# GpSimd instead of SyncE counts the landed row blocks of a graph layer

## The chip, the core and the metric

The kernel runs on one core of a Trainium2 chip. The metric is the device time of one execution in microseconds. A core has five engines with a queue of instructions each: TensorE (matrix products; its weight loads are shown as a unit of their own, PEld), VectorE (DVE), ScalarE (ACT), GpSimd (POOL) and SyncE (SP). They meet only through semaphores: an instruction adds to one, and another engine's queue waits until it holds a value. Transfers (DMA) add 16 to a semaphore when they have landed.

## What is computed

A relational graph layer over 6250 nodes, 200,000 edges and 16 edge types, followed by a layer of 16 experts of which each node takes two:

```python
w_full = jnp.einsum('rb,bdo->rdo', w_comp, weight)
x_rel = jnp.einsum('nd,rdo->rno', feat, w_full)
msg = x_rel[etypes, src] * norm
agg = jax.ops.segment_sum(msg, dst, num_segments=N)
out = agg + h_bias + feat @ loop_weight
return jax.nn.relu(out)
```

Here `feat` is the layer-normed `x` (6250 x 256), `src` and `dst` are the edge's ends, and the edges come sorted by `dst`. The result is added to `x`; the expert layer (gate, top 2 of 16, two products, sum, layer norm) is computed behind it and added in the same way. The change lies in the graph layer.

## The kernel before

The edges are cut into 1568 blocks of 128, the nodes into windows of 16. A step is one block and one window: a matrix `S` with, for each edge and each of the 8 bases, the coefficient of the edge in the column of its node, times the 128 gathered feature rows of the block, added up in a bank of PSUM for the window. There are 1960 steps, seven of which make a turn, so 280 turns.

Each engine has its part of the function `graph_layer`, and they run beside one another:

GpSimd gathers. One indirect DMA (L1069) fetches the 128 feature rows of one block into one of 56 places of a ring in SBUF, `rows`. The first 28 gathers are issued by the stage before the layer, 1540 by the layer itself, in groups of 14 with a list of indices each (L1045), eight groups to a pass of the loop. Ahead of each gather, `landed` (L1047 to L1050) waits until the gather three before it has landed, so no more than three are in flight. The landing semaphores are `s_row`, eight of them in rotation. Then `landed` adds 1 to `s_paced`, which nothing reads. Ahead of each group, L1058 waits until TensorE has done the turns (`s_P`) that read the places to be overwritten.

SyncE first sends for the layer's weights (L1017 to L1022). Then it waits for the row blocks one after the other on the same `s_row` and adds 1 to `s_in` for each (L1025, L1026). Between blocks 392, 616, 896 and 1120 (the third number in `CHUNK`, times 56) it leaves that loop, waits until VectorE has made the `S` of turn 36, 72, 108 or 140 (`s_S`, L1031), and sends for a piece of the late coefficients, 128 rows of 7 or 8 KB (L1033), into the part of `coefS` that those turns have used up. VectorE needs the first of these pieces at turn 141.

VectorE makes four `S` in rotation (L1150), up to three turns ahead of TensorE, and does the layer norm of each tile of 256 nodes that is complete.

TensorE waits per turn for the cleared bank, for `s_in` to reach the last block of the turn (L1275) and for `S` (L1276, L1277), and multiplies (L1278). Where a tile of nodes is complete, it does the tile's product with the basis weights in between (`tile_product`, L1231 to L1244).

ScalarE copies the banks out and clears them, and moves the tiles' rows from and to HBM.

At the end of the layer all engines meet at a barrier (L974), where the slowest is VectorE with the last tile.

Of the kernel before, what the change touches and what calls it, by code (L numbers as in the profile page):

```python
# [38 lines left out]
NBLK = 1568  # L39
# [9 lines left out]
TURNS = STEPS // U  # L49
NS = 4  # L50
# [5 lines left out]
FIRST = TURNS // 2  # L56
LATE = FIRST * U
NEAR = -(-LATE // CS)
CHUNK = [(0, 36, 7), (36, 36, 11), (72, 36, 16), (108, 32, 20)]
assert sum(n for _, n, _ in CHUNK) == TURNS - FIRST and all(n % NS == 0 for _, n, _ in CHUNK) and FIRST % NS == 0  # L60
ZC = B * WIN
BANK = 512
NB = 4
# [15 lines left out]
RB = 56  # L79
GB = 14  # L80
ROWS = 8
AHEAD = 3
IB = 2 * (RB // GB)
EG = 2
CTL_PART = (84, 72, 64, 60)
assert NBLK % RB == 0 and RB % GB == 0 and RB % ROWS == 0 and AHEAD < ROWS and sum(CTL_PART) == TURNS and all(n % NS == 0 for n in CTL_PART)
assert all(t + n <= 8 * i <= TURNS for t, n, i in CHUNK)


SLOTS = (N * K + X * (P - 1)) // P  # L90
# [9 lines left out]
def at_least_one(e, loaded, held):  # L100

    for to, of in zip(held, loaded):
        e.reg_alu(to, of, 1, ALU.max)
    return held
# [74 lines left out]
def later(i):  # L179

    return not isinstance(i, int) or i > 0
# [786 lines left out]
def graph_layer(nc, d, a, ctl, pairs, room, wend, srcT, dstS, wgtS, coefS, ident, wb, lw, hb, gw, s_w, logit, choice, mean, rstd, idx, rows, s_row):  # L968
# [5 lines left out]
    with ctx:  # L974
        def sb(name, shape, dt=F32):
            return ctx.enter_context(nc.sbuf_tensor(name, shape, dt))

        def sem(name):
            return ctx.enter_context(nc.semaphore(name))

        zero = sb("zero", [P, H])
        S = [sb(f"S{h}", [P, U * ZC]) for h in range(NS)]
        z = sb("z", [P, TW * H])
        node = z[:, 0:WIN]
# [15 lines left out]
        node_h = psH[:, 2 * U * WIN:(2 * U + 1) * WIN]  # L1000

        s_in = sem("rows_in")
        s_pool, s_turn, s_paced, s_zr, s_node = sem("pool"), sem("pool_turn"), sem("pool_paced"), sem("zero"), sem("node")
        s_late = [sem(f"late{k}") for k in range(len(CHUNK))]
        s_hot, s_S, s_P, s_clear = sem("hot"), sem("steps_ready"), sem("turn_done"), sem("cleared")
        s_z, s_tp, s_ev = sem("z_done"), sem("tp_done"), sem("tp_out")
# [6 lines left out]
        @blk.sync  # L1013
        def _(e):


            for c in range(HC):  # L1017
                e.dma_start(wb[:, c, :, :], a["L0_gnn_weight"].rearrange("b (c p) o -> c p b o", p=P)[c, :, :, :]).then_inc(s_w, 16)
            e.dma_start(lw[:, :, :], a["L0_gnn_loop_weight"].rearrange("(c p) o -> p c o", p=P)).then_inc(s_w, 16)
            e.dma_start(hb[:, :], a["L0_gnn_h_bias"].partition_broadcast(P)).then_inc(s_w, 16)  # L1020
            e.dma_start(choice[0][:, :], a["L0_ffn_gate_b"].partition_broadcast(P)).then_inc(s_gb, 16)
            e.dma_start(gw[:, :, :], a["L0_ffn_gate_w"].rearrange("(c p) e -> p c e", p=P)).then_inc(s_w, 16)  # L1022
            def rows_in(i):
                for j in range(RB):
                    e.wait_ge(s_row[j % ROWS], i * (RB // ROWS * 16) + (j // ROWS + 1) * 16)  # L1025
                    e.sem_inc(s_in, 1)  # L1026
            i0 = 0
            for k, (t, n, i1) in enumerate(CHUNK):
                with e.Fori(i0, i1) as i:
                    rows_in(i)  # L1030
                e.wait_ge(s_S, t + n)  # L1031
                c = slice(t * U * B, (t + n) * U * B)
                e.dma_start(coefS[:, c], d.coef[:, c]).then_inc(s_late[k], 16)  # L1033
                i0 = i1
            with e.Fori(i0, NBLK // RB) as i:
                rows_in(i)

        @blk.gpsimd
        def _(e):
            ch = Chain(e, s_pool)  # L1040
            regs, room_held = ([e.alloc_register(f"{n}{q}") for q in range(IB)] for n in ("room", "room_held"))
            last = NBLK // (IB * GB) - 1

            def list_in(group, q):
                ch.add(e.tensor_copy(idx[:, q * GB:(q + 1) * GB], srcT[:, bass.ds(group * GB, GB)]))  # L1045

            def landed(i, n):  # L1047

                e.wait_ge(s_row[n % ROWS], i * (IB * GB // ROWS * 16) + (n // ROWS + 1) * 16)
                e.sem_inc(s_paced, 1)  # L1050

            def blocks(i):
                e.load(regs, room[0:1, bass.ds(i * IB, IB)])
                free = at_least_one(e, regs, room_held)
                for q in range(0 if later(i) else EG, IB):
                    if later(i) or q >= RB // GB:

                        e.wait_ge(s_P, free[q])  # L1058
                        e.sem_inc(s_turn, 1)
                    if later(i) or q > EG:  # L1060
                        ch.wait()
                    if q < IB - 1 or not isinstance(i, int) or i < last:
                        list_in(i * IB + q + 1, (q + 1) % IB)
                    else:
                        e.sem_inc(s_turn, 1)
                    for u in range(GB):
                        at = (q * GB + u) % RB
                        landed(i, q * GB + u - AHEAD)
                        e.indirect_dma_start(rows[:, at * H:(at + 1) * H], None, d.feat, bass.IndirectOffsetOnAxis(ap=idx[:, q * GB + u:q * GB + u + 1], axis=0)).then_inc(s_row[at % ROWS], 16)  # L1069
            e.iota(choice[1][:, :], [[1, X]], base=-X, channel_multiplier=0, allow_small_or_imprecise_dtypes=True).then_inc(s_xno, 1)  # L1070
            e.iota(node.rearrange("p (m n) -> p m n", m=2), [[1, 2], [2, WIN // 2]], base=0, channel_multiplier=0, allow_small_or_imprecise_dtypes=True).then_inc(s_node, 1)
            blocks(0)
            with e.Fori(1, last) as i:
                ch.base, ch.n = IB * i - EG, 0
                blocks(i)
            ch.base, ch.n = IB * last - EG, 0
            blocks(last)

        @blk.vector
        def _(e):  # L1080
# [73 lines left out]
            def four(i, t0, c0):  # L1154

                for h0 in range(0, NS, 2):
                    pair(i, t0, c0, h0)
                    if t0:
                        look(i * (NS // 2) + (t0 + h0) // 2)
            four(0, 0, 0)  # L1160
            with e.Fori(0, FIRST // NS - 1) as i:
                four(i, NS, NS)
            for k, (c0, n, _) in enumerate(CHUNK):
                e.wait_ge(s_late[k], 16)
                with e.Fori(0, n // NS) as i:
                    four(i, FIRST + c0, c0)
# [811 lines left out]
def gnn(nc, d, a, ident, sent, got, s_row, logit, choice, mean, rstd):  # L1978
# [3 lines left out]
    with ctx:  # L1982
# [21 lines left out]
        with pre:  # L2004
# [9 lines left out]
            expand(nc, d, wcd, halfs, win_n, ident, tables, wend, pairs, jcol, wcol, spread, dstS, wgtS, coefS, got, s_feat, srcT, idx, rows, s_row)  # L2014
        wb, lw, hb, gw = sb("wb", [P, HC, B, H]), sb("lw", [P, HC, H]), sb("hb", [P, H]), sb("gw", [P, HC, X])
        graph_layer(nc, d, a, ctl, pairs, room, wend, srcT, dstS, wgtS, coefS, ident, wb, lw, hb, gw, s_w, logit, choice, mean, rstd, idx, rows, s_row)


# [54 lines left out]
```

## Time and profile before

| | |
|---|---|
| Median of 3 runs | 2842.06 us (2833.11 to 2845.28) |
| The profiled execution | 2844.61 us |
| Its span, first to last instruction | 2842.7 us |
| TensorE (PE) busy | 2224.4 us, 78% |
| VectorE (DVE) busy | 967.4 us, 34% |
| ScalarE (ACT) busy | 654.3 us, 23% |
| GpSimd (POOL) busy | 1815.4 us, 64% |
| Graph layer | from about 158 us to 2240 us of the span |

Busy time is time in which the engine itself works; instructions of its queue alone (waits, counts on semaphores, branches, the issue of a DMA by SyncE or ScalarE) are not in it. Such instructions carry a q behind the engine's name (SPq, POOLq) and can be listed by their line, with their count and the start of the first and the last. A wait appears as idle time ahead of the next instruction of that engine, put down to the one that ended it; "issue" is idle time for which the profile shows no such one. Times in the views count from the start of the span.

### The profile page before, as it was taken

Reading aid. Unit: us, or ns where it says so; the run is one execution under the profiler, and the core shown is the slowest. Engines: PE = TensorE matmul, PEld = TensorE weight load, DVE = VectorE, ACT = ScalarE, POOL = GpSimd, SP = SyncE. Lnnn points to the kernel's source line nnn. Section 1 sums busy time; section 2 is a strip of 40 time slices with the busy share of each in tenths; the row PEclk is TensorE's granted clock in tenths of the full one; section 3 lists DMA queues with packets and bytes.
Section 4 is the critical chain, followed back from the end, with each engine's and each line's share of the span. In section 5 each row is a group of like instructions: output and inputs, shape, how many; then the busy total and the mean of one; then the engine's idle time right before and its main releaser. Section 6 shows DMA issues by size and latency. Waiting matters only on the chain. (4 is left out here: it accounts for less than half of the span.)

```text
span 2842.7 us, 43421 instructions
## 1 busy us (share of the span) xinstructions
PE 2224.4 (78%) x11549; PEld 1849.9 (65%) x11550; DVE 967.4 (34%) x2172; ACT 654.3 (23%) x1539; POOL 1815.4 (64%) x2000
## 2 busy tenths in 40 slices
PE   1779999999988888876776768557655579999987
PEld 0567787877776666664664646445444379999975
DVE  6733333342332322222222212112112453333347
ACT  2522323232222211111110101001000233333345
POOL 0557777777777777777777777777777035555544
PEclk9999999999999989998898878789777799999998
DMA  6544444344333434334333333333333552222246
GB/s 210 160 146 119 121 118 123 116 120 134 116 117 111 129 111 116 111 112 122 109 109 109 118 107 108 108 100 114 103 103 94 187 182 70 70 70 70 70 131 220
DMA packets 146270, 338.66 MB, mean 119 GB/s; under 512 B 36674, under 2 KB 56290, under 8 KB 146051
## 3 DMA queue, kind: packets, MB, share of 16 engines
q0 software_dynamic: 89296, 245.33, 29.5%
q1 hardware_dynamic: 39311, 59.54, 6.1%
q10 hardware_dynamic: 17588, 32.88, 3.5%
q8 instruction: 36, 0.59, 0.1%
q14 instruction: 39, 0.32, 0.0%
HBM read 292.84 MB, written 47.97 MB: 120 GB/s over the span
## 5 line engine op out<-in xcount | busy, mean ns | idle before, releaser
L1069 POOL DMA_INDIRECT rows<-feat,idx x1540 | 1468.1, 953 | 548.9 <-issue 462.5
L1278 PE MATMUL psW<-rows,S 128*128 x3920 | 1065.1, 433 | 413.8 <-SPq L1026 380.8
L1278 PEld LDWEIGHTS psW<-rows,S 128*128 128x128 f32 x3920 | 842.1, 219 | 632.7 <-issue 495.0
L1150 DVE TENSOR_TENSOR S<-psHere,coefS 128x896 f32<-128x896 f32 x280 | 301.6, 1090 | 1379.0 <-PE psW L1278 1372.4
L1338 ACT COPY z<-psW 128x512 f32<-128x512 f32 x196 | 114.9, 586 | 1461.3 <-PE psW L1278 1460.6
L1244 PE MATMUL psG<-wb,zT 128*128 128x256 f32 (+1 forms) x1600 | 353.5, 379 | 0.0
L1244 PEld LDWEIGHTS psG<-wb,zT 128*128 128x128 f32 (+1 forms) x1600 | 300.6, 188 | 44.7
L1729 PE MATMUL psH<-xT,w1x 128*128 128x128 f32 x1840 | 226.8, 277 | 0.3
L1680 POOL DMA_INDIRECT expert_rows<-os,at_rows x114 | 114.0, 1000 | 171.3 <-DVE os L1788 171.3
L1729 PEld LDWEIGHTS psH<-xT,w1x 128*128 128x128 f32 x1840 | 216.5, 193 | 2.0 <-issue 1.9
L1738 PE MATMUL psO<-w2s,hT 128*128 x912 | 215.7, 379 | 0.0
L1702 ACT ACTIVATE hT<-psH,b1T 128x128 f32<-128x128 f32 x460 | 131.5, 368 | 315.6 <-PE psH L1729 315.6
L1676 POOL DMA_INDIRECT xs<-y_rows,at_rows x116 | 115.0, 991 | 100.7 <-POOLq L1408 56.6
L1738 PEld LDWEIGHTS psO<-w2s,hT 128*128 128x128 f32 x912 | 164.6, 190 | 17.6
L1788 DVE TENSOR_TENSOR os<-psO,b_b 128x256 f32<-128x256 f32 x114 | 48.4, 425 | 236.9 <-PE psO L1738 236.4
L1231 PE MATMUL psZ<-ident,z 128*128 128x128 f32 x784 | 113.8, 283 | 13.5 <-ACT zT L1352 8.8
L1340 ACT COPY psW<-zero 128x512 f32<-128x512 f32 x196 | 115.6, 590 | 6.2
L1352 ACT COPY zT<-psZ 128x512 f32<-128x512 f32 x196 | 108.1, 589 | 18.4 <-PE psZ L1231 18.4
L1231 PEld LDWEIGHTS psZ<-ident,z 128*128 128x128 f32 x784 | 83.7, 141 | 36.1 <-ACT zT L1352 20.1
L1772 DVE COPY w1x<-w1s 128x1024 f32 x116 | 86.1, 742 | 0.0
L1898 PE MATMUL psSum<-g,dg 128*128 128x256 f32 x200 | 56.0, 405 | 17.3 <-DMA g<-expert_rows 17.1
L1141 DVE TENSOR_TENSOR psHere<-dstS,psHere 128x224 f32<-128x224 f32 (+1 forms) x140 | 55.3, 395 | 31.5 <-DVE S L1150 25.1
(284 smaller groups left out, 1442.1 us busy)
## 6 DMA issues: line engine op xcount, KB each, us to landing
rows<-feat,idx POOLq DMA_INDIRECT x1568
g<-expert_rows SPq DMA_DIRECT2D x24, 512.0 KB, 5.5
w1s<-in_L_ffn_w SPq DMA_DIRECT2D x8, 1024.0 KB, 10.0
w2s<-in_L_ffn_w SPq DMA_DIRECT2D x16, 512.0 KB, 10.1
feat<-rows SPq DMA_DIRECT2D x24, 256.0 KB, 3.0
fts<-feat ACTq DMA_DIRECT2D x24, 256.0 KB, 2.8
h<-in_x ACTq DMA_DIRECT2D x24, 256.0 KB
y_rows<-y ACTq DMA_DIRECT2D x24, 256.0 KB
```

What stands on the lines that cost most here:

```text
L1069: e.indirect_dma_start(rows[:, at * H:(at + 1) * H], None, d.feat, bass.IndirectOffsetOnAxis(ap=idx[:, q * GB + u:q * GB + u + 1], axis=0) ...
L1150: e.tensor_tensor(S[h0 + h][:, :].rearrange("p (s b n) -> p s b n", s=U, b=B), both[:, h * U:(h + 1) * U, :].unsqueeze(2).to_broadcast([P, ...
L1231: last = e.transpose(to[:, k * P:(k + 1) * P], z[:, w * H + c * P:w * H + (c + 1) * P], ident[:, :])
L1244: last = e.matmul(psG[0:Q, m * H:(m + 1) * H], zT[:, at:at + Q], wb[:, c, b, :], start=False, stop=(c == HC - 1 and b == B - 1))
L1278: last = e.matmul(psW[:, bass.ds(bank[u], H)], S[h][:, u * ZC:(u + 1) * ZC], rows[:, bass.ds(slot[u], H)], start=False, stop=True, skip_gr ...
L1338: e.copy(z[:, 2 * k * H:2 * (k + 1) * H], bank).then_inc(s_z, 1)
L1340: e.copy(bank.rearrange("p (w o) -> p w o", w=2), zero[:, :].unsqueeze(1).to_broadcast([P, 2, H])).then_inc(s_clear, 1)
L1676: e.indirect_dma_start(xs[n % XS][:, :], None, d.y, bass.IndirectOffsetOnAxis(ap=at_rows[:, n, 0:1], axis=0)).then_inc(s_in[n % XS], 16)
L1680: e.indirect_dma_start(d.two, bass.IndirectOffsetOnAxis(ap=at_rows[:, n + 4, 1:2], axis=0), os_[n % 2][:, :], None).then_inc(s_out[n % 2], 16)
L1702: last = e.activation(hT[k][:, c * P:(c + 1) * P], psH[k][:, c * P:(c + 1) * P], ACT.Relu, bias=b1T[:, bass.ds(ex * FC + c, 1)])
L1729: last = e.matmul(psH[k][:, f * P:(f + 1) * P], w1x[k][:, c * F + f * P:c * F + (f + 1) * P], xT[k][:, c * P:(c + 1) * P], start=(c == 0), ...
L1738: last = e.matmul(psO[k][:, 0:H], hT[k][:, c * P:(c + 1) * P], w2s[:, bass.ds(ex, 1), c, :].rearrange("p e f -> p (e f)"), start=(c == 0), ...
```

## The change

The order of the counts moves. `landed` on GpSimd adds to `s_in` instead of `s_paced`, which goes. Since `landed` begins with block 25, GpSimd counts the 25 blocks before that ahead of its first list, and the last three behind its last gather. SyncE keeps the weights and the four loads of late coefficients, each of which it issues as soon as VectorE has made the `S` of the turn in question; the third number of `CHUNK` goes with the loops.

```diff
-CHUNK = [(0, 36, 7), (36, 36, 11), (72, 36, 16), (108, 32, 20)]
+CHUNK = [(0, 36), (36, 36), (72, 36), (108, 32)]
...
-            def rows_in(i):
-                for j in range(RB):
-                    e.wait_ge(s_row[j % ROWS], i * (RB // ROWS * 16) + (j // ROWS + 1) * 16)
-                    e.sem_inc(s_in, 1)
-            i0 = 0
-            for k, (t, n, i1) in enumerate(CHUNK):
-                with e.Fori(i0, i1) as i:
-                    rows_in(i)
+            for k, (t, n) in enumerate(CHUNK):
                 e.wait_ge(s_S, t + n)
                 c = slice(t * U * B, (t + n) * U * B)
                 e.dma_start(coefS[:, c], d.coef[:, c]).then_inc(s_late[k], 16)
-                i0 = i1
-            with e.Fori(i0, NBLK // RB) as i:
-                rows_in(i)
...
                 e.wait_ge(s_row[n % ROWS], i * (IB * GB // ROWS * 16) + (n // ROWS + 1) * 16)
-                e.sem_inc(s_paced, 1)
+                e.sem_inc(s_in, 1)
...
+            for n in range(EG * GB - AHEAD):
+                landed(0, n)
             blocks(0)
...
             blocks(last)
+            for n in range(IB * GB - AHEAD, IB * GB):
+                landed(last, n)
```

## Rows read from the trace of the kernel before

**Rows 1.** The page: its first line.

```profile
span 2842.7 us, 43421 instructions
```

**Rows 2.** Busy time by stretch: length, engines' busy us (instructions), TensorE clock, DMA, GB/s.

```profile
157.00:500.00 343.00, 312.63 (x1527) 260.72 (x1528) 117.30 (x267) 104.37 (x188) 244.33 (x274) 1.00 0.42 124
...
1500.00:2203.00 703.00, 444.27 (x1531) 346.71 (x1529) 150.92 (x251) 44.91 (x81) 519.53 (x574) 0.81 0.37 106
```

**Rows 3.** Waits of TensorE: who waited, for whom, us in total, times, longest.

```profile
PE psW L1278 <- SPq L1026: 380.8, 132, 7.8
```

**Rows 4.** Waits of SyncE's queue.

```profile
SPq L1026 <- DMA rows<-feat,idx: 1960.8, 1539, 4.7
...
SPq L974 <- DVEq L974: 36.2, 1, 36.2
```

**Rows 5.** Waits of GpSimd, 157 to 2260 us.

```profile
POOL rows L1069 <- issue: 462.5, 1422, 3.4
POOL rows L1069 <- DMA rows<-feat,idx: 85.6, 116, 4.6
...
POOL rows L1069 <- PE psW L1278: 0.8, 2, 0.5
```

**Rows 6.** Gathers: line view (ns min/median/max, first and last start); one in the timeline.

```profile
L1069 POOL DMA_INDIRECT rows<-feat,idx x1540: 943/949/1541, 159.5 to 2199.5; - x193
...
1501.70 0.95 POOL L1069 DMA_INDIRECT rows<-feat,idx  x1 [0.30 <-issue]
```

**Rows 7.** Counts of SyncE (L1026) and GpSimd (L1050), line views, 1500 to 1510 us.

```profile
L1026 SPq EVENT_SEMAPHORE  x8: 17/17/17, 1500.7 to 1509.6; - x8
L1050 POOLq EVENT_SEMAPHORE  x8: 17/17/17, 1500.7 to 1509.6; - x8
```

**Rows 8.** Counts of the same block by both: the first and the last late pair.

```profile
L1026 SPq EVENT_SEMAPHORE  x1: 17/17/17, 172.1 to 172.1; - x1
L1050 POOLq EVENT_SEMAPHORE  x1: 17/17/17, 172.5 to 172.5; - x1
...
L1026 SPq EVENT_SEMAPHORE  x1: 17/17/17, 1997.1 to 1997.1; - x1
L1050 POOLq EVENT_SEMAPHORE  x1: 17/17/17, 1999.2 to 1999.2; - x1
```

**Rows 9.** A count by GpSimd at a landing that held it, and the gather behind.

```profile
L1050 POOLq EVENT_SEMAPHORE  x1: 17/17/17, 171.9 to 171.9; - x1
...
172.69 0.95 POOL L1069 DMA_INDIRECT rows<-feat,idx  x1 [1.63 <-DMA rows<-feat,idx]
```

**Rows 10.** SyncE's counts: all, and the first 28; GpSimd's first and fourth gather.

```profile
L1026 SPq EVENT_SEMAPHORE  x1568: 17/17/17, 164.2 to 2203.3; - x196
L1026 SPq EVENT_SEMAPHORE  x28: 17/17/17, 164.2 to 166.3; - x28
...
159.49 1.00 POOL L1069 DMA_INDIRECT rows<-feat,idx  x1 [0.57 <-issue]
...
167.61 0.95 POOL L1069 DMA_INDIRECT rows<-feat,idx  x1 [4.61 <-DMA rows<-feat,idx]
```

**Rows 11.** Line view of the layer's end: GpSimd's drain.

```profile
L974 POOLq DRAIN  x1: 6357/6357/6357, 2199.2 to 2199.2; - x1
```

**Rows 12.** VectorE's `S`, line view, up to 379.5 us and up to 1048.4 us.

```profile
L1150 DVE TENSOR_TENSOR S<-psHere,coefS x36: 1080/1092/1093, 160.9 to 378.1; 128x896 f32<-128x896 f32 x36
L1150 DVE TENSOR_TENSOR S<-psHere,coefS x140: 1080/1092/1093, 160.9 to 1047.2; 128x896 f32<-128x896 f32 x140
```

**Rows 13.** The four late loads, line view; the gather held behind the first and fourth.

```profile
L1033 SPq DMA_DIRECT2D coefS<-late_coefs x4: 320/323/331, 649.0 to 1617.0; - x4
...
655.61 0.95 POOL L1069 DMA_INDIRECT rows<-feat,idx  x1 [3.30 <-DMA rows<-feat,idx]
...
1622.62 0.94 POOL L1069 DMA_INDIRECT rows<-feat,idx  x1 [1.91 <-DMA rows<-feat,idx]
```

More of the change, by code:

```diff
@@ L58 @@
 NEAR = -(-LATE // CS)
-CHUNK = [(0, 36, 7), (36, 36, 11), (72, 36, 16), (108, 32, 20)]
-assert sum(n for _, n, _ in CHUNK) == TURNS - FIRST and all(n % NS == 0 for _, n, _ in CHUNK) and FIRST % NS == 0
+CHUNK = [(0, 36), (36, 36), (72, 36), (108, 32)]
+assert sum(n for _, n in CHUNK) == TURNS - FIRST and all(n % NS == 0 for _, n in CHUNK) and FIRST % NS == 0
 ZC = B * WIN
@@ L86 @@
 assert NBLK % RB == 0 and RB % GB == 0 and RB % ROWS == 0 and AHEAD < ROWS and sum(CTL_PART) == TURNS and all(n % NS == 0 for n in CTL_PART)
-assert all(t + n <= 8 * i <= TURNS for t, n, i in CHUNK)
 SLOTS = (N * K + X * (P - 1)) // P
@@ L1002, in graph_layer @@
         s_in = sem("rows_in")
-        s_pool, s_turn, s_paced, s_zr, s_node = sem("pool"), sem("pool_turn"), sem("pool_paced"), sem("zero"), sem("node")
+        s_pool, s_turn, s_zr, s_node = sem("pool"), sem("pool_turn"), sem("zero"), sem("node")
         s_late = [sem(f"late{k}") for k in range(len(CHUNK))]
@@ L1162, in _ @@
                 four(i, NS, NS)
-            for k, (c0, n, _) in enumerate(CHUNK):
+            for k, (c0, n) in enumerate(CHUNK):
                 e.wait_ge(s_late[k], 16)
```

## The prediction

> **What bounds the kernel now.** Read the span first: 2842.7 us [rows 1]. The profiled execution took 2844.61 us, so 1.91 us lie around the span; the median of the runs is 2842.06 us, 2.55 us below that execution. The change lies in the graph layer alone, so the second view is the table by stretches [rows 2]. In the layer's first part TensorE is busy 312.6 of 343 us, in its last part 444 of 703; GpSimd is busy 71% and 74%. No engine is full in the later part, so the reader has to ask who waits for whom.
>
> The waits answer that. TensorE's row multiplications waited 380.8 us in 132 pieces for the counter on SyncE, L1026 [rows 3]. SyncE in turn waited 1539 times, 1960.8 us in all, for a gather to land [rows 4]; it is therefore never behind: with 1568 counts, all but 29 find it waiting already. So the counter passes on what arrives, and what arrives is set by the gathers. Who sets the gathers? GpSimd's own line says it: 462.5 us of idle time before 1422 gathers came with no wait that the profile can name, 85.6 us before 116 of them with a landing, and 0.8 us before 2 with TensorE having to free room in the ring [rows 5]. A gather takes 0.95 us on GpSimd and 0.30 us pass before the next: a beat of 1.25 us, 1540 times, is 1925 us of the 2040 us from the first gather of the layer to its last [rows 6]. GpSimd's beat paces the layer; TensorE follows it; SyncE only reports.
>
> **The counts themselves.** The decisive question is whether GpSimd is at its wait for a row block before that block lands, or comes later. If it came later, TensorE would hear of every block later than now. GpSimd already waits for each landing three gathers behind and counts it in one instruction on its queue (L1050, 1540 of them, 17 ns each), only into a semaphore that nobody reads. So both engines' counts of the same blocks can be laid side by side. Over ten microseconds in the middle both show 8 counts with the same first and last tenth [rows 7]. Event by event over the layer, GpSimd's count stands 7 or 8 ns behind SyncE's in 1447 of 1540 cases. The queue runs ahead of the engine: while the engine still works on one gather, the queue already stands at the wait ahead of the next. 84 counts are over 50 ns late, because the queue was then held by the copy of an index list, a wait for room or the loop's turn; they sum to 66 us, and 27 of them, 15 us, lie before 700 us; the first and the last of the 84 are shown [rows 8].
>
> Changing the target of these 1540 instructions removes nothing from GpSimd's queue and adds nothing. Does the queue have air if such an instruction cost a little more? A count at 1500.7 is followed by its gather at 1501.70, 1.0 us later, with the engine busy in between; where the landing itself held GpSimd, the gather started 0.75 to 0.8 us after the count (171.9, then 172.69) [rows 6, 7, 9]. So about 0.2 us per gather are hidden behind the engine's own beat. I take zero.
>
> The Trainium skill speaks against this edit: "Trainium Kernel Development and Optimization", section NeuronCore Architecture, lists barriers and semaphore operations as SyncE's work and custom operations as GpSimd's, by which counting would be taken from GpSimd's gathers. The trace does not agree here, as the 1540 counts are already on GpSimd's queue; by the rule the sum would be that of the third rival below.
>
> **What the late counts cost.** TensorE hears of those 84 blocks later, on average 0.8 us. That is a delay, not a loss of rate: the next blocks are counted on time again, GpSimd waits for TensorE in 2 of 1540 cases [rows 5], and a turn that starts 1 us late is caught up in the next wait. I take zero, with 15 us as the upper bound for the stretch where TensorE is nearly full.
>
> **The new instructions.** GpSimd gets 25 counts ahead of its first list and 3 behind its last gather. SyncE did its first 28 counts in 164.2 to 166.3 us, 0.078 us each [rows 10]; 25 of them are 2.0 us on GpSimd's queue ahead of the first gather at 159.49. That is hidden if the fourth gather does not move: it started at 167.61 after a landing wait of 4.61 us [rows 10], because the first three gathers were in flight beside 2 MB of weights that SyncE had just sent for. The cover is twice as long as the 2.0 us. If the first landing moves along, 2.0 us are paid. I take zero, nearest to the row with the wait, and keep +2.0. The 3 counts at the end come when the landings come, the last at 2203.3 [rows 10], after which TensorE's last turn starts as now. GpSimd's end-of-layer drain of 6.36 us [rows 11] can begin only then, and would end near 2209.7; SyncE waits at that barrier 36.2 us for VectorE [rows 4], so some 30 us of cover remain.
>
> **What leaves SyncE.** 1568 counts and the loops around them. They took nothing from others, except that TensorE's first turn could not start before 164.2. It may start about a microsecond earlier, and that goes into its next wait.
>
> **The four loads.** Now SyncE is free to send for the 1 MB coefficient blocks as soon as their place is free: turns 36, 72, 108 and 140. VectorE has made 36 of its tiles by 379 us and 140 by 1048 us [rows 12]; the loads now go at 649.0, then to 1617.0 [rows 13]. Each takes the path that the gathers take: the gather behind the first stood idle 3.30 us, behind the fourth 1.91, against 0.30 usually [rows 13, 6]; the two between stood 2.96 and 2.28. The four together cost 9.3 us of GpSimd's beat now. Moved 270 to 570 us earlier they cost about the same, on other gathers, and nobody waits for them, since the first is needed at turn 141. Bounds: nothing at all if each falls into a pause that is there anyway, -9.3 us; or 4 times the longest landing wait of 4.6 us [rows 5], 18.4 us, so +9.1. I take zero.
>
> **Sum.** Counts 0, late counts 0, new instructions 0 (to +2.0), SyncE 0, loads 0 (-9.3 to +9.1): 2844.6 us for an execution like the profiled one, 2842 us for the median.
>
> **The rivals.** (1) Slower: late counts reach the end. Place: the stretch to 500 us, where TensorE is 91% busy [rows 2] and the ring has least room to spare. A TensorE turn that starts late frees its slots late, GpSimd waits for room, and the delay enters the beat. Price: the 15 us of late counts before 700 us, 2857 us; were TensorE the pacer throughout, all 66 us, 2908 us. It decides from the point where GpSimd's waits for TensorE are more than those 0.8 us. Against it: just that number. (2) The moved loads decide: 2833 to 2851 us; either end is inside half a per cent. For a loss speaks that the early stretch carries more transfers for finished tiles, against it that a gather held by one transfer hides another. (3) GpSimd's counting costs its gathers time once another engine listens: 17 ns by 1540 counts, 26 us, 2868 us; more only if a count exceeds the 0.2 us of air. Against it: the same instruction stands in the same place today. (4) Faster: the loads' pauses vanish, 2833 us; over 0.5% would need 14.2 us, and the rows offer no more than 9.3.
>
> **How the numbers follow.** Half a per cent, 14.2 us, is about what a measurement of this kernel can tell from no change. Forecast of no change, with the second rival inside it: 0.88. First rival 0.05, third 0.04: slower 0.09. Faster by over 0.5%: 0.03, for something the rows don't show. Range: below, 2842 minus 9.3 and a little for the spread of the runs shown (2833 to 2845), 2831; above, 2842 plus 2.0, 9.1 and a little for that spread, which is also the first rival's lower price, 2857.
>
> **What would show it.** Right: GpSimd's counting line holds 1568 instructions; gathers keep 0.95 us and 0.30 us; TensorE's wait of about 380 us stands, now with GpSimd's queue as its releaser; the last gather of the layer stays near 2199 us; four loads between about 380 and 1050 us, each with a pause of 2 to 3 us. Wrong: gaps of more than 0.30 us before most gathers (rival 3), GpSimd waiting for TensorE by tens of microseconds (rival 1), or landing waits that grow or shrink by more than 9 us (loads). The forecast would fall with any cost of the 1540 redirected counts above 0.2 us each.

## The result and the profile after

The changed kernel is slower: 2886.59 us in the median of 4 runs (2884.7 to 2888.23), beside 2843.45 for the kernel before. The ratio is 1.0157, with a 95% interval of 1.0135 to 1.018. The forecast was no change, 2842 us in a range to 2857; the time lies 30 us above that range. The profiled execution took 2885.13 us, its span is 2883.4 us, 40.7 us more than before [rows 1].

The first view is again the table by stretches, with the same columns and limits as [rows 2]:

```profile
157.00:500.00 343.00, 314.59 (x1539) 262.66 (x1538) 115.44 (x261) 104.55 (x189) 239.62 (x267) 0.99 0.42 124
500.00:1000.00 500.00, 434.56 (x2053) 359.72 (x2051) 164.17 (x377) 126.89 (x228) 352.87 (x394) 0.98 0.40 118
1000.00:1500.00 500.00, 382.23 (x1630) 310.09 (x1630) 126.01 (x268) 84.43 (x153) 352.43 (x392) 0.90 0.38 110
1500.00:2203.00 703.00, 443.95 (x1522) 346.51 (x1522) 144.44 (x252) 46.82 (x85) 513.21 (x572) 0.81 0.36 104
```

GpSimd gets through fewer instructions in each stretch: 267, 394, 392 and 572, where it was 274, 402, 404 and 574. In the last stretch, which reaches to 2203 us, the kernel before had already issued its last gather and the kernel after had not. The loss is spread over the layer. The line views say how much of it there is: the counts now all stand on GpSimd's line, the last gather starts at 2239.0 instead of 2199.5 [rows 6], and the loads go between 376.7 and 1067.2:

```profile
L1039 POOLq EVENT_SEMAPHORE  x1568: 17/17/17, 154.5 to 2243.0; - x196
L1058 POOL DMA_INDIRECT rows<-feat,idx x1540: 940/946/1539, 158.6 to 2239.0; - x193
L1025 SPq DMA_DIRECT2D coefS<-late_coefs x4: 320/324/327, 376.7 to 1067.2; - x4
```

A gather still takes 0.95 us. So the 40 us lie between gathers. The waits of GpSimd, 157 to 2300 us, and TensorE's wait for the count, as in [rows 5] and [rows 3]:

```profile
POOL rows L1058 <- issue: 479.5, 1424, 3.4
POOL rows L1058 <- DMA rows<-feat,idx: 86.3, 116, 4.0
...
POOL idx L1034 <- issue: 30.5, 11, 3.3
POOL idx L1034 <- PE psW L1271: 2.9, 1, 2.9
...
PE psW L1271 <- POOLq L1039: 414.7, 138, 8.6
```

Landings hold GpSimd as long as before (86.3 against 85.6 us, 116 times both). TensorE waits 34 us longer, as an engine does that follows a slower one. What is new is the third line: ahead of the copy of an index list GpSimd stood idle 11 times, 30.5 us in all, for nothing that the view can name, and "issue" ahead of gathers grew by 17 us. Placed in the timeline, one of the eleven is the first list, behind the 25 new counts; the other ten each stand behind a jump back of GpSimd's loop. The loop has 12 passes and jumps back 11 times: behind the remaining jump the view puts the same idle time, 2.9 us, down to TensorE (the fourth line). The timeline shows one such place, first of the kernel after, then the same turn of the loop in the kernel before:

```profile
1644.18 0.95 POOL L1058 DMA_INDIRECT rows<-feat,idx  x1 [0.30 <-issue]
1648.25 0.19 POOL L1034 COPY idx<-srcT 128x14 int32 x1 [3.13 <-issue]
1650.16 0.98 POOL L1058 DMA_INDIRECT rows<-feat,idx  x1 [1.72 <-issue]
```

```profile
1614.01 0.95 POOL L1069 DMA_INDIRECT rows<-feat,idx  x1 [0.30 <-issue]
1615.14 0.20 POOL L1045 COPY idx<-srcT 128x14 int32 x1 [0.18 <-issue]
1615.97 0.98 POOL L1069 DMA_INDIRECT rows<-feat,idx  x1 [0.64 <-DMA rows<-feat,idx]
```

From the last gather of a pass to the first of the next it is 1.96 us before and 5.98 us after. The line views of GpSimd's queue narrow it to one step, the loop's branch (first start in us; L1064 after, L1073 before):

```profile
L1064 POOLq COMPARE_BRANCH  x1: 53/53/53, 1643.9 to 1643.9; - x1
L1064 POOLq FUSED_REGOPS  x1: 68/68/68, 1647.0 to 1647.0; - x1
```

```profile
L1073 POOLq COMPARE_BRANCH  x1: 53/53/53, 1613.7 to 1613.7; - x1
L1073 POOLq FUSED_REGOPS  x1: 68/68/68, 1613.9 to 1613.9; - x1
```

Between the branch and the first instruction at its target lie 0.2 us before and 3.1 us after, with no semaphore in between; over all 11 jumps it is 0.3 us before and 2.5 to 3.5 us after. One line of the pages' queue table, that of the kernel before and then that of the kernel after, points to what GpSimd waits for (packets, MB):

```profile
q14 instruction: 39, 0.32, 0.0%
```

```profile
q14 instruction: 92, 0.75, 0.1%
```

53 more packets of 8 KB on a queue that carries instructions. By their times in the trace four or five of them start within about 9 us of each jump back (at 1642.0, 1645.4, 1647.7 and 1650.3 us around the jump shown), and another about half a pass later. Laid gather by gather beside the kernel before, the first gathers behind the 11 jumps come 40.1 us later, and all other gathers together 0.6 us earlier. The whole loss is at the jumps: 3.6 us each.

### The profile page after: what moved, and what is told of

Read it like the earlier page. It is cut to its first block and busy times, and to the rows that moved or that the text cites. A ratio compares the mean times of both kernels' runs of the same rounds, so it can differ in the third digit from the quotient of the medians.

```text
span 2883.4 us, 41624 instructions
## 1 busy us (share of the span) xinstructions
PE 2233.3 (77%) x11549; PEld 1855.0 (64%) x11550; DVE 966.7 (34%) x2172; ACT 654.3 (23%) x1539; POOL 1810.0 (63%) x2000
## 5 line engine op out<-in xcount | busy, mean ns | idle before, releaser
L1271 PE MATMUL psW<-rows,S 128*128 x3920 | 1075.9, 437 | 446.3 <-POOLq L1039 414.7
L1224 PEld LDWEIGHTS psZ<-ident,z 128*128 128x128 f32 x784 | 83.8, 141 | 36.1 <-ACT zT L1345 20.1
## 6 DMA issues: line engine op xcount, KB each, us to landing
w2s<-in_L_ffn_w SPq DMA_DIRECT2D x16, 512.0 KB, 10.1
```

The source lines that it names most:

```text
L1224: last = e.transpose(to[:, k * P:(k + 1) * P], z[:, w * H + c * P:w * H + (c + 1) * P], ident[:, :])
L1271: last = e.matmul(psW[:, bass.ds(bank[u], H)], S[h][:, u * ZC:(u + 1) * ZC], rows[:, bass.ds(slot[u], H)], start=False, stop=True, skip_gr ...
```

## The experiments

Four theories stood after this. Place: 25 new instructions ahead of GpSimd's loop move the loop in instruction memory, so that its start is no longer held when it jumps back. Count: TensorE served by GpSimd's counts is what costs. Loads: the four earlier loads cost. Length: each added instruction on GpSimd's queue costs. The table stands ahead of the single runs:

| kernel | counts for TensorE | instructions ahead of the list | jumps back | packets on q14 | ratio to before (95%) |
|---|---|---|---|---|---|
| before | SyncE | 0 | 11 | 39 | 1 |
| b_p12 | SyncE | 12 | 11 | 39 | 1.0002 (0.9992 to 1.0011) |
| b_p25 | SyncE | 25 | 11 | 94 | 1.0145 (1.0126 to 1.0164) |
| b_p40 | SyncE | 40 | 11 | 39 | 1.0 (0.999 to 1.001) |
| b_p153 | SyncE | 153 | 11 | 95 | 1.016 (1.0143 to 1.0177) |
| after | GpSimd | 25 | 11 | 92 | 1.0157 (1.0135 to 1.018) |
| a_loadslate | GpSimd | 25 | 11 | 92 | 1.0151 (1.0133 to 1.0169) |
| a_half | GpSimd | 25 | 5 | 74 | 1.0066 (1.0049 to 1.0083) |
| a_inc25 | GpSimd | 1 | 11 | 37 | 1.0 (0.9988 to 1.0012) |

**b_p25: the kernel before with the 25 instructions alone.**

```diff
+            for n in range(25):
+                landed(0, n % (EG * GB - AHEAD))
             blocks(0)
```

> The kernel before, with 25 waiting counts into the semaphore that nobody reads put ahead of GpSimd's first list; SyncE still counts for TensorE and the loads keep their times. Place theory: the 25 instructions shift GpSimd's loop in instruction memory so that each of its 11 jumps back fetches its instructions anew, some 3.7 us each: ratio to before 1.014 (about 2885 us), some 50 more 8 KB packets on the instruction queue than the 39 of before. Count theory (TensorE served by GpSimd's counts is what costs): ratio 1.000, 2843 us. Load theory (the four loads moved earlier are what costs): 1.000. Length theory (every added instruction on GpSimd's queue costs): 1.014, as the place theory.

2884.22 us, ratio 1.0145. With counts and loads as in the kernel before, GpSimd's waits take the pattern of the kernel after:

```profile
POOL rows L1069 <- issue: 479.8, 1431, 3.0
POOL rows L1069 <- DMA rows<-feat,idx: 79.4, 107, 4.1
...
POOL idx L1045 <- issue: 32.7, 11, 3.5
```

As in the kernel after, one of the 11 is the first list and ten are jumps. So the 25 instructions carry the whole loss, and the count and load theories fall as its cause. Place and length are still both alive.

**b_p40: 40 instead of 25.** The same edit with `range(40)`.

> As the kernel before with 40 of those waiting counts ahead of GpSimd's first list instead of none. Place theory: the loop's start has been pushed past the next multiple of 128 instructions, it fits again, ratio 1.000 (2843 us, at most 3 us more for the 40 counts themselves) and about 39 packets on the instruction queue. Length theory: more than with 25, ratio 1.02 (41 us by 40/25 is 66 us, 2909 us). Count and load theories: 1.000.

2842.63 us, ratio 1.0, 39 packets. More instructions cost nothing where fewer cost 41 us; length falls. GpSimd's waits are those of the kernel before again:

```profile
POOL rows L1069 <- issue: 466.8, 1434, 3.5
POOL rows L1069 <- DMA rows<-feat,idx: 82.9, 104, 3.6
```

**a_inc25: the changed kernel with one instruction that adds 25 in place of the 25.**

```diff
-            for n in range(EG * GB - AHEAD):
-                landed(0, n)
+            e.sem_inc(s_in, EG * GB - AHEAD)
             blocks(0)
```

> The changed kernel, with the 25 waiting counts ahead of GpSimd's first list replaced by one instruction that adds 25; GpSimd had waited for those 25 blocks in the stage before. All else of the change stays: GpSimd counts for TensorE, the loads go early. Place theory: the loop stands one instruction behind where it stood before, ratio to before 1.000 (2843 us), about 39 packets on the instruction queue, no fetch at the jumps back. Count theory: 1.015 (2886 us). Load theory: 1.015. Length theory: 1.001.

2842.86 us, ratio 1.0 (0.9988 to 1.0012). GpSimd counts for TensorE, the loads go early, and nothing is lost. TensorE waits 365.4 us for the counts, and by the line view the last gather starts at 2196.3 us:

```profile
PE psW L1270 <- POOLq L1039: 365.4, 133, 7.3
```

```profile
POOL rows L1058 <- issue: 464.4, 1422, 3.2
POOL rows L1058 <- DMA rows<-feat,idx: 85.4, 115, 4.5
```

```profile
L1058 POOL DMA_INDIRECT rows<-feat,idx x1540: 940/947/1541, 157.7 to 2196.3; - x193
```

**a_loadslate: the changed kernel with the loads held back.**

```diff
-                e.wait_ge(s_S, t + n)
+                e.wait_ge(s_S, (77, 121, 177, 213)[k])
```

> The changed kernel with the four loads of late coefficients held back to about the times that they had before (after VectorE's turns 77, 121, 177 and 213 instead of 36, 72, 108 and 140). Place theory: nothing changes for GpSimd's loop, ratio to before 1.015 (2886 us), some 92 packets on the instruction queue. Load theory: ratio 1.000 (2843 us). Count theory: 1.015.

2885.1 us, ratio 1.0151, with the loads at 629.0 to 1635.6 us, near their old times. Their place makes no difference that can be measured, neither for good nor for ill.

**b_p153: 128 more than 25.** The edit of b_p25 with `range(153)`.

> The kernel before with 153 waiting counts ahead of GpSimd's first list, 128 more than the 25 that cost 41 us; 40 cost nothing. Place theory with blocks of 128 instructions (8 KB packets of the instruction queue, one per some 128 instructions of GpSimd's queue in the unrolled parts): the loop stands again as with 25, ratio to before 1.014 to 1.017 (41 us for the jumps back, and up to 8 us for 153 counts at 0.07 us each where the wait for the first landing doesn't cover them), some 90 packets on the instruction queue. If what counts is only that the loop starts beyond some place, so that 40 and more are always free: 1.000 to 1.003.

2884.8 us, ratio 1.016, 95 packets. The loss returns, 39.7 us of it at the 11 jumps. The counts themselves hold up the first list by 15.7 us, most of which shorter landing waits give back (70.6 us instead of 85.6). So it isn't a matter of being beyond some place, but of the place within a block of 128 instructions: what 25 cost, 153 cost.

**b_p12: fewer than 25.** The same edit with `range(12)`.

> The kernel before with 12 waiting counts ahead of GpSimd's first list. In the trace of before the last fetch inside the loop's first pass stands about 108 instructions ahead of the pass's end, so the next would come 20 instructions behind it. Place theory: 12 fit, ratio 1.000, about 39 packets on the instruction queue. A cost that grows with the count up to 25: 41 us by 12/25, ratio 1.007.

2839.63 us, ratio 1.0002. No gradual cost: the step lies between 12 and 25, where the reading of the packets' times had put it, at about 20.

**a_half: the changed kernel with half the jumps.**

```diff
-            with e.Fori(1, last) as i:
-                ch.base, ch.n = IB * i - EG, 0
-                blocks(i)
+            with e.Fori(0, (last - 1) // 2) as j:
+                for h in (1, 2):
+                    ch.base, ch.n = IB * (j * 2 + h) - EG, 0
+                    blocks(j * 2 + h)
```

> The changed kernel, with GpSimd's loop of 12 passes written as 6 passes of twice the length, so that it jumps back 5 times instead of 11; the work is the same. Place theory: each jump back still misses, since the body is longer than what is kept, and costs 3.7 us: 5 x 3.7 = 19 us, ratio to before 1.0065 (2863 us). If the cost lies in something else of the changed kernel (counting by GpSimd, loads): 1.015 as the changed kernel.

2858.3 us, ratio 1.0066. Beside the kernel before, the first gathers behind the 5 jumps come 19.5 us later, 3.9 us each; at the six places where a jump was taken away they come 1.6 us earlier in all. One of the jumps, in the timeline:

```profile
571.75 0.95 POOL L1058 DMA_INDIRECT rows<-feat,idx  x1 [0.30 <-issue]
576.96 0.19 POOL L1034 COPY idx<-srcT 128x14 int32 x1 [4.27 <-issue]
577.85 0.98 POOL L1058 DMA_INDIRECT rows<-feat,idx  x1 [0.70 <-issue]
```

The price is one of jumps, not of the loop's work, which is the same.

**Five gathers in flight, and seven.** The view of GpSimd's waits had shown 85.6 us of landing waits behind a limit of three gathers in flight [rows 5]. That is a part of the layer's time that neither the beat of the gathers nor the loop explains, and with the loop back in its place it could be tried: a_inc25 with `AHEAD = 5`, then `AHEAD = 7`, and the kernel before with `AHEAD = 5`.

```diff
-AHEAD = 3
+AHEAD = 5
```

> The changed kernel with one instruction that adds the first blocks, and five gathers in flight instead of three ahead of GpSimd's wait. The loop keeps its place (ratio 1.000 by that alone). Waits for a landing stopped GpSimd for 85 us before 116 gathers; with five in flight most of these should be covered: if all 85 us go, ratio 0.970 (2758 us); if transfers are merely pushed together and later ones land later, 0.985 to 1.000.

> The kernel before with five gathers in flight instead of three; SyncE counts for TensorE at the landing, the loads keep their times. If the gain of 2.3% that five in flight gave with GpSimd counting is the gathers' alone: ratio to before 0.977 (2776 us). If GpSimd's counting costs something once it comes up to five gathers behind the issue, so that TensorE hears of a block later, the kernel with SyncE's counting is faster: 0.970 or less. If GpSimd's counting or the early loads helped: 0.980 or more.

> The changed kernel with one instruction for the first blocks and seven gathers in flight, the most that eight landing semaphores allow. With five, 21 us of landing waits were left on GpSimd. If these go and nothing else comes: ratio 0.970. If TensorE becomes the next to be late (with five GpSimd waited 23 us for room in the ring, up to 9 us at once, since GpSimd's counts come later and the ring fills): 0.975 to 0.980.

With five, GpSimd counting: 2775.47 us, 0.9773 (0.9757 to 0.979). With five, SyncE counting: 2777.42 us, 0.9773 (0.9757 to 0.9789). With seven, GpSimd counting: 2773.24 us, 0.9756 (0.974 to 0.9773). GpSimd's waits in the first of the three, 157 to 2250 us:

```profile
POOL rows L1058 <- issue: 439.5, 1475, 1.3
...
POOL idx L1034 <- PE psW L1270: 22.8, 4, 9.0
POOL rows L1058 <- DMA rows<-feat,idx: 21.4, 63, 1.9
```

Landing waits fall from 85 to 21 us, "issue" ahead of gathers by another 25 us, and GpSimd now waits 22.8 us in 4 pieces for TensorE to free the ring. The gain, 64 to 69 us between the medians of each comparison, lies for the first run between the two ends of its expectation. Five and seven differ by less than their intervals; with seven the waits for room are 24.8 us and those for landings 20.1 us, so by these views the next thing in the way is TensorE as much as the landings. And the two kernels with five are alike, one with counts at the landing, one with counts that GpSimd makes up to five gathers behind: who counts does not show even there. With SyncE counting, the waits for room are 23.4 us, so they don't come from GpSimd's later counts, as the expectation for seven had it. All three beat both kernels of this case.

## Why the prediction was wrong, point by point

**What paces the layer** was right. Every loss and gain went through GpSimd's beat: 40 us at its jumps back became 40.7 us of span, and with five in flight 64 us of landing waits and 25 us of "issue" less, with some 21 us more of waits for room, became 64 us of time. TensorE's wait for counts grew and shrank behind it (380.8, 414.7, 365.4 us) without any say.

**The counts, at zero,** were right: a_inc25 moves all of them and stays within 0.12% of before, 3.4 us, less than the 15 us of the first rival and the 26 us of the third. The division of labour in the Trainium skill ("Trainium Kernel Development and Optimization", NeuronCore Architecture), which would have given the third rival, finds nothing here to bear it out. Idle "issue" time did grow, which would have misled a reader who stops at that line into the third rival: but it grew at the jumps, not ahead of most gathers, which was that rival's sign.

**The late counts, at zero,** were right by the same run. In the kernel after some counts come still later, those at a jump, and the only wait of GpSimd's for TensorE that the views show there, 2.9 us, stands behind a jump, where the other ten have as much without it. (The 84 late counts run on to 2134.5 us; the pair at 1997.1 us in [rows 8] is a late one, not the last.)

**The loads, at zero,** were right. After 376.7 us and the three later issues the gathers stood idle 2.99, 2.21, 2.20 and 2.64 us, 8.8 us beyond the usual 0.30 (10.1 us with a second wait of 1.58 us behind the third), against 9.3 before, counted in the same way; a_loadslate differs from the changed kernel by less than its interval.

**The new instructions, at 0 to +2.0 us,** is the step that failed. As work they cost no more than the bound, though the cover that was to hide them did not hold: they put 2.4 us ahead of the first list (3.13 instead of 0.74 us), and the landing wait of the fourth gather shrank by 0.6 us only, from 4.61 [rows 10] to 4.00. From GpSimd's first instruction of the layer to the fourth gather it is 11.6 us where it was 9.9, so 1.8 us were paid; the layer began 3.3 us earlier in that execution, which hides it. Here are GpSimd's first instruction and first list, before, and then the same with the fourth gather, after:

```profile
157.74 0.15 POOL L1070 IOTA xno<- 128x16 f32 x1 [12.43 <-POOLq L656]
...
158.72 0.20 POOL L1045 COPY idx<-srcT 128x14 int32<-128x14 int32 x1 [0.74 <-issue]
```

```profile
154.47 0.15 POOL L1059 IOTA xno<- 128x16 f32 x1 [8.36 <-POOLq L655]
...
157.84 0.20 POOL L1034 COPY idx<-srcT 128x14 int32<-128x14 int32 x1 [3.13 <-issue]
...
166.10 0.94 POOL L1058 DMA_INDIRECT rows<-feat,idx  x1 [4.00 <-DMA rows<-feat,idx]
```

What the step left out is that 25 instructions also take up room, and that a loop stands behind them. The prediction listed the queues that a moved step passes, and took an instruction's cost to be its time. The price of the place, 40 us, appeared in no term, no bound and no rival; the chance of 0.09 for slower was given to other mechanisms. It could have been read from the trace of before. A pass of the loop has some 270 instructions of GpSimd's queue, 112 of them gathers; ahead of the loop and in its first pass packets of 8 KB come about every 128 instructions (at the 186th, 314th and 443rd of GpSimd's events); in the later passes none comes at a place that repeats from pass to pass. The loop is held, then, in three such blocks, and its last instruction stood some 20 ahead of the next block's fetch. 25 were to be put ahead of it.

**What the runs show and what they don't.** Shown: the loss comes with the place alone (b_p25, a_inc25), returns after 128 instructions (b_p153), is absent at 0, 1, 12 and 40, and is paid per jump, 3.6 to 3.9 us (40.1 us over 11 jumps in the kernel after, 42.7 in b_p25, 39.7 in b_p153, 19.5 over 5 in a_half). The traces give the places as well. Up to the first jump back, packets come at about the 186th, 314th, 443rd, 570th and 699th of GpSimd's events, whatever stands ahead of the loop. The loop's 271 events run from the 279th to the 549th in the kernel before; with 1, 12 and 40 instructions ahead they end at the 550th, 561st and 589th. Each of these four loops has two of the packets' places inside. With 25 it runs from the 304th to about the 574th, with 153 from the 432nd to about the 702nd, and has three. Inferred from this: a body of 2.1 blocks that touches three is kept, one that touches four is not, because the block ahead is fetched over the one that holds the loop's start. How many blocks are kept, and in what order they are replaced, no run here tells apart. In all kernels with the loss the loop also starts at the same place in a block, near its end; that its end in a fourth block counts, and not this start, is not shown by a run.

The Trainium skill has the rule that was wanted: "Runtime: NRT & Kernel Launch", section Instruction fetch mechanics, says that a taken branch whose target is outside the window of instructions held forces a fetch before the engine goes on. The trace agrees, with 3.1 us between branch and target where 0.2 us stood before. The page gives refills in blocks of 16 KiB, 256 instructions; by that b_p153 would not stand where b_p25 stands, and it does. Here the packets are of 8 KB and the period fits 128 instructions, and the measurement decides.

## What to carry to other kernels

Instructions put ahead of a long loop move it, and where an engine's loop is about as long as what its queue holds, the place alone can decide whether each jump back fetches the loop anew: look at the packets of the instruction queue and at the gap between a loop's branch and the instruction behind it, before and after. If a small edit off the path costs much more than its own time, lay the two traces side by side by the loop's pass; a loss that sits at one place of every pass is not that of the edited work. A test of place is cheap: the same number of idle instructions in the old kernel, then some more.

## What the runs showed of the hardware that was not expected

- A jump back to a loop of some 270 instructions on GpSimd's queue took 0.3 us or 2.5 to 3.7 us from the branch to its target, by where the loop stood; over a pass, with what follows from it, the difference was 3.6 to 3.9 us.
- The fetches went in packets of 8 KB: 37 to 39 on that queue in the kernels without the loss, 92 to 95 in those with it and 11 jumps, 74 with 5 jumps.
- Two engines that wait for the same landing see it 7 to 8 ns apart in 1447 of 1540 cases, and it made no difference to the time which of them passes it on.
- A fourth and fifth gather in flight took three quarters of the landing waits away (85.4 us in a_inc25 to 21.4 us).
